# Attention periods of a fused layer kernel: three steps of the hand-written order moved

## The reference, cut to what matters

```python
q = (x @ Wq).reshape(B, S, H, hd)            # 16 heads of 16
kv_latent = x @ Wkv                           # width 64
k, v = kv_latent @ Wk, kv_latent @ Wv
mask = (ki <= qi) & ((qi - ki < 128) | (ki < 16))
attn = softmax(where(mask, q @ k.T * hd ** -0.5, min))
x = x + (attn @ v) @ Wo
```

## Time and profile before

| | |
|---|---|
| median of 3 runs | 772.26 us (767.83 to 773.0) |
| the profiled execution, its span | 766.56 us, 764.8 us |
| mean granted TensorE clock | 0.871 |
| PE busy | 618.8 us (81%) |
| DVE, ACT, POOL busy | 465.6 (61%), 296.7 (39%), 342.0 us (45%) |

### The profile page before, as it was taken

How to read it: one execution, slowest core, us unless ns; L and a number is a source line. 1 busy time by engine, 2 the same in 40 slices (tenths; PEclk the granted TensorE clock), 3 DMA queues, 4 the chain that set the end, 5 groups by cost and what they waited for, 6 DMA issues and landing times. The chain is left out here.

```text
span 764.8 us, 14771 instructions
## 1 busy us (share of the span) xinstructions
PE 618.8 (81%) x4827; PEld 479.8 (63%) x4827; DVE 465.6 (61%) x1226; ACT 296.7 (39%) x567; POOL 342.0 (45%) x400
## 2 busy tenths in 40 slices
PE   1789999995639999964569999999988769999950
PEld 0667787774535767743457787877866545777740
DVE  6994858869435534456365766787786544644422
ACT  1363435152002444444134545555454413444420
POOL 4304040723531667755332444345557650653435
PEclk9998989896666999986658999999999756999985
DMA  8599500132011453327435246403501512443328
GB/s 274 201 351 351 184 1 0 45 90 74 22 61 56 145 168 98 100 79 239 62 69 85 57 105 150 95 24 78 107 17 46 135 53 58 145 135 100 99 93 295
DMA packets 68318, 86.94 MB, mean 114 GB/s; under 512 B 8909, under 2 KB 62802, under 8 KB 67380
## 3 DMA queue, kind: packets, MB, share of 16 engines
q1 hardware_dynamic: 61428, 67.80, 32.7%
q0 software_dynamic: 6816, 18.19, 6.7%
HBM read 35.13 MB, written 39.06 MB: 97 GB/s over the span
## 5 line engine op out<-in xcount | busy, mean ns | idle before, releaser
L1295 POOL DMA_INDIRECT back<-f_yout,f_target x78 | 76.9, 985 | 113.2 <-ACT f_yout L1402 102.6
L1337 PE MATMUL bank<-f_wgu,f_xt 128*128 x312 | 113.5, 488 | 3.4 <-ACT f_xt L1387 3.3
L1184 POOL DMA_INDIRECT xs<-xn,f_slots x64 | 65.2, 1018 | 57.3 <-ACT xn L1175 41.7
L1442 DVE TENSOR_TENSOR f_hid<-f_act_g,bank 128x176 f32<-128x176 f32 x78 | 26.4, 338 | 104.3 <-ACT f_act_g L1394 100.2
L1359 PE MATMUL bank<-f_wd,f_hT 88*128 x312 | 81.5, 385 | 0.0
L2069 POOL TENSOR_SCALAR_AFFINE_SELECT b_prob<-b_prob 128x512 f32<-128x512 f32 x60 | 38.4, 640 | 92.6 <-ACT b_prob L2310 92.3
L2310 ACT ACTIVATE b_prob<-bank 128x1024 f32<-128x1024 f32 x60 | 61.5, 1024 | 46.2 <-PE bank L2149 45.9
L1337 PEld LDWEIGHTS bank<-f_wgu,f_xt 128*128 128x128 f32 x312 | 59.2, 199 | 31.1 <-issue 9.4
L2379 DVE COPY_PREDICATED bank<-b_later,bank 128x512 f32<-128x512 int32 x60 | 41.6, 694 | 33.5 <-PE bank L2119 30.1
L1359 PEld LDWEIGHTS bank<-f_wd,f_hT 88*128 88x128 f32 x312 | 54.2, 193 | 4.8
L1402 ACT ACTIVATE f_yout<-bank,f_share 128x256 f32<-128x256 f32 x78 | 37.0, 474 | 39.8 <-PE bank L1359 38.9
(11 more groups left out here) (313 smaller groups left out, 1475.4 us busy)
## 6 DMA issues: line engine op xcount, KB each, us to landing
xs<-xTf SPq DMA_DIRECT2D x8, 2176.0 KB, 19.2
f_xin<-xs SPq DMA_DIRECT2D x78, 136.0 KB, 2.1
f_wgu<-in_wgu SPq DMA_DIRECT2D x4, 1408.0 KB, 6.0
f_wgu<-back SPq DMA_DIRECT2D x16, 256.0 KB, 5.6
b_KS<-b_kh SPq DMA_DIRECT2D x32, 128.0 KB, 4.1
b_QS<-b_qh SPq DMA_DIRECT2D x32, 128.0 KB, 3.8
f_back<-back SPq DMA_DIRECT2D x8, 512.0 KB, 8.5
f_wd<-in_wd SPq DMA_DIRECT2D x4, 968.0 KB
```

What stands on the lines that cost most here:

```text
L1184: pool.indirect_dma_start(m.xs, bass.IndirectOffsetOnAxis(m.slots[:, g, c, i:i + 1], 0), xn[:, g * TPC + i], None)\
L1295: pool.indirect_dma_start(m.back, bass.IndirectOffsetOnAxis(target[:, g % AR:g % AR + 1], 0), yout[:, g % YB], None, bounds_check=2 * 2 * ...
L1337: mm = pe.matmul(psG[:, g % 2, 0:2 * FH], xt[:, g % 2, k * P:(k + 1) * P], m.gu[:, k, bass.ds(e, 2 * FH)], start=k == 0, stop=k == KD - 1)
```

## The change

Three moves in the order, on the engines that they concern; no instruction is added, taken away or changed.

1. The projection of step 2 (key, value; in period 0 the query's) goes from the end of the step to directly behind scores_persist, ahead of transposed(b, 1) and values(b, 0). ScalarE's copy of it goes ahead of the step's exponential. VectorE's rest keeps its place.
2. out_transposed goes from step 3 to step 4, ahead of tail_transposed; out_high likewise, ahead of tail_high.
3. out_low(n - 3) of step 4 becomes out_low(n - 4) of step 0 of the next period, behind maxima(n, 0).

```diff
@@ -2260,6 +2260,8 @@
                             scores(n, QUAD_AT[u])
                         if 1 <= n < NB and u == 2:
                             scores_persist(n)
+                        if u == 2 and (n, u) in PROJ:
+                            project_task(pe, *PROJ[n, u])
                         if 0 <= b < NB and u > 0:
                             transposed(b, u - 1)
                         if u == 1 and 0 <= b < NB:
@@ -2274,13 +2276,13 @@
                             project_out(b - 2)
                         if u == 1 and 0 <= n - 3 < NB:
                             values_back(n - 3)
+                        if u == 4 and 0 <= n - 3 < NB:
+                            out_transposed(n - 3)
                         if u == 4 and 0 <= n - 4 < NB:
                             tail_transposed(n - 4)
-                        if u == 3 and 0 <= n - 3 < NB:
-                            out_transposed(n - 3)
                         if u >= 3 and 0 <= b < NB:
                             values(b, u - 2)
-                        if (n, u) in PROJ:
+                        if u != 2 and (n, u) in PROJ:
                             project_task(pe, *PROJ[n, u])
                         if (n, u) in PAIRS:
                             pair_transposed(pe, PAIRS[n, u])
@@ -2344,6 +2346,8 @@
                 for n in range(PERIODS):
                     b = n - LEAD
                     for u in range(NSTEP):
+                        if u == 2 and (n, u) in PROJ:
+                            high_task(act, *PROJ[n, u])
                         if 0 <= b < NB:
                             if u > 0:
                                 expo(b, u - 1)
@@ -2351,19 +2355,19 @@
                                 expo_persist(b)
                         if u == 0 and 0 <= b - 1 < NB:
                             values_out(b - 1)
+                        if u == 4 and 0 <= n - 3 < NB:
+                            out_high(n - 3)
                         if u == 4 and 0 <= n - 4 < NB:
                             tail_high(n - 4)
                         if turned is not None and turned + 1 < NHC:
                             pair_norm(act, turned + 1)
                         turned = PAIRS.get((n, u))
-                        if (n, u) in PROJ:
+                        if u != 2 and (n, u) in PROJ:
                             high_task(act, *PROJ[n, u])
                         if turned is not None:
                             pair_high(act, turned)
                         if u == 1 and 0 <= n - 1 < NB:
                             max_out(n - 1)
-                        if u == 3 and 0 <= n - 3 < NB:
-                            out_high(n - 3)
                         if (n, u) in RANKS:
                             act_counts(act, m, 1, RANKS[n, u], psJ[:, 3 * P:4 * P])
                         if (n, u - 1) == LATE_LOGITS:
@@ -2441,6 +2445,8 @@
                             maxima_joined(n)
                         if 1 <= n < NB and u == 2:
                             maxima_persist(n)
+                        if u == 0 and 0 <= n - 4 < NB:
+                            out_low(n - 4)
                         if u == 0 and n % 2 == 0 and (n, 0) in PROJ:
                             low_task(dve, *PROJ[n, 0])
                         if u == 1 and n % 2 == 1 and (n, 0) in PROJ:
@@ -2454,11 +2460,8 @@
                                 tail_norm(n - 4)
                         if u == 3 and (n, 2) in PROJ:
                             low_task(dve, *PROJ[n, 2])
-                        if u == 4:
-                            if 0 <= n - 3 < NB:
-                                out_low(n - 3)
-                            if (n, u) in PROJ:
-                                low_task(dve, *PROJ[n, u])
+                        if u == 4 and (n, u) in PROJ:
+                            low_task(dve, *PROJ[n, u])
                         if turned is not None:
                             pair_low(dve, turned)
                         turned = PAIRS.get((n, u))
```

## The result

The changed kernel takes **824.17 us** (median of 4 runs, 816.3 to 832.15) where the kernel before takes 770.35: 1.071 times as long, with an interval of 1.064 to 1.078. I had forecast 798 and 780 to 812. The direction is right, the size is half of what came: 54 us instead of 26. The ratios and the last table leave out executions over 1.5% above the fastest of their kernel, the medians have all; of four kernels the profiled execution is one of those left out, so no rows of them stand here.

What follows compares the result with a forecast made beforehand. It took TensorE's in-order queue to bound the attention stage; 14.5 + 3.4 + 8.0 = 25.9, or 26 us, on a median of 772.3 gave 798 us, range 780 to 812.

Steps and rivals of the forecast that it cites:

- Part A: Step 0, periods 4 to 15: the output projection waits for out_low, now behind the maxima on VectorE; 14.5 us slower.
- Part B: The output's two transposes in step 4 delay the next step 0's scores by 0.38 us in nine periods; 3.4 us.
- Part C: Step 2's projection ahead of the transposed scores delays the chain to the values of step 3; 8.0 us slower.
- a bound: Step 2: no loss from the moved projection if TensorE's row groups let it and the transposed scores run into each other.
- a sign that it is wrong: The granted clock's row falling below 1.00 between 420 and 580 would show the forecast wrong.
- the rival's 828: Clock falls: a fifth of twelve periods' TensorE work at half the clock adds 30 us, giving 828; chance 0.08.

Runs made afterwards that it cites:

- part C alone: The kernel before with only the projection of step 2 and ScalarE's copy of it moved directly behind the persistent scores; 778.69 us, 1.016.
- the stop of A filled: The changed kernel plus ten unread matmuls ahead of the output projection's wait in each of periods 4 to 15; 806.05 us, 1.053.
- the control with fillers: The kernel before plus ten unread matmuls ahead of the output projection in periods 4 to 15, where it has no stop; 778.44 us, 1.014.
- part A filled: The kernel before with only out_low moved behind the maxima of step 0, plus ten unread matmuls ahead of the output projection; 783.68 us, 1.020.
- both filled: The changed kernel plus ten unread matmuls ahead of the output projection and five ahead of the values of step 3; 792.6 us, 1.033.

## Why the prediction was wrong, and where it was right

**Part A** was costed at 14.5 us and comes to 15.1 in the table. The place, the chain and the size were right. In period 5 the stop is 1.10 and the projection is 2.35 - 1.21 = 1.14 us later, a little less than the 1.29 that I had for it, since out_low starts 0.08 before the end of the reduction in the rows, where I had 0.04 behind it; twelve matmul stops sum to 11.9 us in the waits, and the weight loads see more.

**Part B** was costed at 3.4 and comes to 1.3. The ratio alone, 0.2 to 1.2% or 1.6 to 9.2 us, can't tell the two apart.

**Part C** was costed at 8.0 and comes to 5.6, so it was put too high. Period 4 of the changed kernel, steps 2 to 4, which answers to the earlier trace rows:

```profile
436.31 0.38 PE L1752 MATMUL bank<-b_lath,b_bkh 64*128 64x256 f32 x1
...
436.78 0.33 PE L2149 MATMUL bank<-b_QS,b_KS 64*128 64x128 f32 x1
...
437.01 0.28 PE L1752 MATMUL bank<-b_latl,b_bkh 64*128 64x256 f32 x1
...
437.32 0.60 ACT L1788 ACTIVATE b_kh<-bank 128x512 fp32r<-128x512 f32 x1 [1.48 <-PE bank L1752]
...
437.82 1.02 ACT L2312 ACTIVATE b_prob<-bank 128x1024 f32<-128x1024 f32 x1
...
438.89 0.66 PE L2149 MATMUL bank<-b_QS,b_KS 64*128 64x128 f32 x8 [0.21 <-ACT b_prob L2312]
...
439.50 0.64 POOL L2071 TENSOR_SCALAR_AFFINE_SELECT b_prob<-b_prob 128x512 f32<-128x512 f32 x1
...
440.19 0.63 PE L2190 MATMUL bank<-b_prob,b_V 128*17 128x128 f32 x16 [0.64 <-POOL b_prob L2071]
...
440.75 0.51 PE L2119 MATMUL bank<-b_KS,b_QS 48*128 48x256 f32 x4
...
441.58 0.44 PE L2222 MATMUL bank<-ident_sb,b_on 128*128 128x128 f32 x2
```

The projection starts at 436.31, directly behind the persistent scores. The transposed scores begin at 436.78, while matmuls of the projection still start (the last at 437.01), so the projection delays them by 0.47 instead of the 0.75 that I took: the two run into each other in part, which I had named as a bound and not counted. The prediction puts it to TensorE's row groups, which no trace shows as such; what they show is that matmuls over 64 and over 48 partitions start side by side. In period 7 of the kernel before the last of the value projection start at 473.82, 473.94 and 474.06, scores of step 3 among them at 473.83, 474.05 and 474.18, and the projection's stay 0.12 us apart, as they were without the scores (473.59 to 473.71). ScalarE's copy (437.32) holds the exponential until 437.82, as costed. Then TensorE stops 0.21 ahead of the transposed scores of step 3 and 0.64 ahead of its values. The scores of step 4 start 440.75 - 436.31 = 4.44 us behind the start of the projection (4.43 in the kernel of part C alone); I had 4.53, and 3.89 for the kernel before.

So the sum of the waits, 25.9, came out at 22.9. **The step that failed** is the clock, which the sum took to hold, at a cost of nothing; the reason stands in the rivals: "The new stops come once or twice a period in a queue that stays over 80% busy, which is nearer to the first. ... Chance 0.08." What the runs showed in its place: 106 us more at the lower clock, worth 33 us, more than the waits themselves. The clock's row fell below 1.00 between 420 and 580, which the prediction had named as a sign that it is wrong. That the rival's 828 is so near the 824 is in part luck: a fifth of twelve periods' work at half the clock is some 60 us at the lower clock, each costing 0.5, which makes 30; it was 106 us, each costing 0.31.

I had read the single stop of 1.37 us in period 14, after which the clock stayed at 1.00, as evidence that stops of that size are harmless. One stop that passed says little of two or three in each of twelve periods. The same stops bring 0.57 in period 5 of the changed kernel, after period 4 passed with them at 1.00; with the stop of A filled, one of 0.63 us brings 0.53. Nor does the busy share tell it: period 14 of the kernel before, as a whole, was at 83% (11.50 of 13.86 us) and held its clock, about the share of period 4 of the changed kernel (12.26 of 14.39, 85%):

```profile
559.32:573.18 13.86, 11.50 (x172) 8.97 (x165) 11.75 (x28) 6.37 (x13) 7.75 (x13) 1.00 0.06 22
```

So the trace of before held one instance in favour of the forecast and none that could bound the rival; its chance had to be far higher than 0.08, and the range had to reach it. These runs show that waits of TensorE between matmuls can bring the lower clock, and that short ones do: 0.63 us for GpSimd, with 0.53 behind it, and 1.10 us for VectorE, with 0.57.

I can't say from these runs why a given stop brings the clock down and the next does not. The stop of period 10 is the plainest case: 0.84 us in the kernel before and 1.13 in the control with fillers, both at 1.00 throughout; 0.82 in part C alone, 1.13 in part A filled and in the changed kernel with the stop of A filled, 1.14 with both filled, and each time the clock fell within some 2 us behind it (windows of 1 us: 0.67 from 518, 0.98 from 520, 0.55 from 533 and 0.97 from 525, each with 0.50 in the next, behind 516.36, 518.58, 531.62 and 524.93).

## What to carry to other kernels

In a stage where TensorE is busy nearly without a break, cost a new stop twice: its own length, and the stretch at the lower clock that may follow; here the second was the larger, 33 us of 56. A high busy share after the change is no sign against that, since at the lower clock the same matmuls fill more time (here 4.00 of 4 us at 0.57): compare the matmuls done per us, and the clock's column. And before moving an operation "one step later", find its reader: in the queue of the other engine it may stand in that very step, ahead of what the operation now has to queue behind.

## What I had not expected of the hardware

Work for nothing that makes a kernel faster: 120 matmuls took the changed kernel from 1.071 to 1.053 of the kernel before, 170 to 1.033, without one wait made shorter. And stops of 0.6 to 1.1 us are enough for the lower clock to come back in some periods (0.53 from 468 to 472, behind a stop of 0.63; 0.57 from 446 to 450, behind one of 1.10), while a stop of 1.37 us in the kernel before was not.
